# Two expert layers of a metaformer block: weights moved to the stationary side of TensorE, pooled tokens to the moving side

## What is computed

```
probs = softmax(logits, axis=1)                       # over the tokens
vals, idx = top_k(probs.transpose(0, 2, 1), K)        # each expert takes 8 tokens
pooled = einsum('bked,bke->bed', gathered, topv)      # one vector of 64 per image and expert
h = concatenate([pooled.transpose(1, 0, 2), ones], -1)
h = gelu(einsum('ebd,edh->ebh', h, weight1))          # weight1 is (32, 65, 256), last row the bias
h = concatenate([h, ones], -1)
out = einsum('ebh,eho->ebo', h, weight2)              # weight2 is (32, 257, 64), last row the bias
outputs = scatter_add(weighted by topv)
```

## Time and profile before

| | us |
|---|---|
| median of 3 runs | 206.62 (203.53 to 207.08) |
| the profiled execution | 206.30 |
| its span, first to last instruction | 204.5 |
| mean granted TensorE clock in it | 0.981 of full |
| first product of layer 1 | 178.23 |
| first `o_n` (line 918) | 186.37 |
| last DVE add ends (line 930) | 197.7 |

### The profile page before, as it was taken

One profiled execution on the slowest core, in us unless ns is written; L12 is line 12 of the kernel. 1 busy time (PEld: TensorE's weight loads), 2 busy tenths in 40 slices (PEclk: granted clock), 3 DMA queues, 4 the chain that ended last, 5 costly groups with the idle time before them and its releaser, 6 DMA issues.

```text
span 204.5 us, 10877 instructions
## 1 busy us (share of the span) xinstructions
PE 178.7 (87%) x4687; PEld 147.9 (72%) x4687; DVE 164.3 (80%) x605; ACT 109.9 (54%) x266; POOL 125.5 (61%) x113
## 2 busy tenths in 40 slices
PE   1789996999999989999999999999997988998900
PEld 1578875799869978987999798888874776684200
DVE  0768797999999898899889968888889999445960
ACT  2373435665666555667556566666457696640000
POOL 4443549598987989698898899579248930000000
PEclk9999999999999999999999999999999999999975
DMA  4955090422423143251441342432180131000896
GB/s 104 186 111 109 10 199 11 107 58 58 102 59 84 33 104 103 62 103 33 133 108 34 83 106 58 118 98 56 53 194 19 51 107 51 6 3 8 232 350 235
DMA packets 29120, 19.12 MB, mean 94 GB/s; under 512 B 2464, under 2 KB 28048, under 8 KB 29072
## 3 DMA queue, kind: packets, MB, share of 16 engines
q1 hardware_dynamic: 27440, 15.87, 31.1%
q10 hardware_dynamic: 1632, 2.56, 4.1%
HBM read 14.12 MB, written 4.30 MB: 90 GB/s over the span
## 4 chain that ended last, share of the span: by engine, by line
PE 63%; DVE 18%; issue 5%; POOL 4%; DMA 2%; ACT 2%; SPq 1%; DVEq 0%; POOLq 0%
PE ps L946 42%; PE ps L937 10%; PE ps L1006 4%; POOL r L404 3%; DMA w_rows<-in_L_conv_w_stos 2%; PE ps L1073 2%; DVE ps L715 2%; DVE tail_room L930 2%; DVE xtok L930 2%; DVE lg L871 2%; DVE x_split L866 2%; DVE st L674 2%; DVE cands L860 1%; PE ps L1194 1%; PE ps L1238 1%
## 5 line engine op out<-in xcount | busy, mean ns | idle before, releaser
L946 PE MATMUL ps<-x_split,w_hi 64*64 64x256 f16 x1000 | 50.3, 273 | 2.0 <-DVE fc L718 1.1
L382 POOL TENSOR_TENSOR xc<-xc,h 128x256 f32<-128x256 f32 x31 | 22.6, 728 | 22.8 <-DVE h_lo L699 22.8
L946 PEld LDWEIGHTS ps<-x_split,w_hi 64*64 64x64 f16 x1000 | 25.9, 107 | 13.5 <-issue 8.7
L715 DVE TENSOR_TENSOR ps<-sg_i,ps 64x256 f32<-64x256 f32 x62 | 26.6, 430 | 8.8 <-ACT ps L515 7.3
L946 PE MATMUL ps<-h_hi,w_lo 64*64 64x256 f16 x750 | 32.4, 272 | 0.8 <-issue 0.8
L946 PE MATMUL ps<-h_lo,w_hi 64*64 64x256 f16 x750 | 32.2, 272 | 0.0
L946 PE MATMUL ps<-h_hi,w_hi 64*64 64x256 f16 x750 | 32.1, 272 | 0.0
L499 ACT ACTIVATE ps<-ps,bias 128x256 f32<-128x256 f32 x32 | 14.3, 448 | 32.8 <-PE ps L946 32.8
L404 POOL TENSOR_TENSOR r<-v,pow_exp 128x16 f32<-128x16 f32 x7 | 20.6, 2936 | 8.5 <-DVE v L668 8.5
L946 PE MATMUL ps<-x_split,w_lo 64*64 64x256 f16 x500 | 24.9, 270 | 0.0
L937 PE MATMUL ps<-ident,xc 128*128 128x128 f32 x128 | 18.5, 289 | 6.9 <-DMA xc<-in_x 5.4
(11 more groups left out here) (130 smaller groups left out, 329.8 us busy)
## 6 DMA issues: line engine op xcount, KB each, us to landing
xc<-in_x SPq DMA_DIRECT2D x14, 256.0 KB, 4.0
rb_xr<-scratch SPq DMA_DIRECT2D x14, 256.0 KB, 4.4
w1s<-in_L_ffn_weight SPq DMA_DIRECT2D x8, 256.0 KB, 3.6
w2s<-in_L_ffn_weight SPq DMA_DIRECT2D x8, 256.0 KB, 3.2
rbf<-scratch SPq DMA_DIRECT2D x24, 64.0 KB, 2.4
out<-xtok SPq DMA_DIRECT2D x4, 256.0 KB, 5.4
out<-xtok ACTq DMA_DIRECT2D x4, 256.0 KB, 5.9
out<-tail_room SPq DMA_DIRECT2D x3, 256.0 KB, 4.4
```

The lines of the kernel that those rows point to most:

```text
L382: p.tensor_tensor(here, here, h32[:, i % 2, :].rearrange("p (b w) -> p b w", w=W), ALU.add) \
L715: v.tensor_tensor(ps_ig[half(h), :], sg_i[half(1 - h), :], pre[G][half(1 - h), 0:COLS], ALU.mult) \
L946: ins = pe.matmul(pre[gate][to, 0:COLS], w[half(h), tap, C * GATE_ORDER[gate]:][:, 0:C], data[half(h)], start=first and m == 0, stop=s_don ...
```

## The change

- **Layer 1** (line 1198 of the changed kernel): an expert's weights, 64 rows by 128 columns (every second one of the 256 hidden units, `m::2`), are loaded; its 16 pooled tokens move. 64 products instead of 32. The hidden values come out already turned: hidden unit on the partitions.
- The gelu writes straight into `hid_t`, 128 x 256 at a time for two halves' worth of experts. No turns of the hidden values and no DVE copies follow.
- **Layer 2** (line 1205): the weights, 128 rows by 64 columns, are loaded; 16 hidden columns move. The 16 products of one k (8 experts) all write the same 64 partitions, `half(k % 2)`; the next k writes the other 64.
- Both biases are products with `row_expert` moving (`first_bias`, now 128 columns, and the new `second_bias`); `b2`, its turn and its copy are gone.
- Pooled tokens are copied in two parts: groups 0 to 2 by ACT from one bank, group 3 by DVE from another. `pool_t` is no longer padded; its zeroing on POOL becomes a zeroing of `o_t`.
- DVE copies layer 2's result to `o_t` in four parts, and the four last turns become four products with `ident2` (two stacked 64 x 64 identities, made on POOL), which add up the two halves.
- SP issues the loads of `b1_rows` and `b2_rows`, now four each, after the LSTM and ahead of the last five pieces of expert weights.

```diff
             for g in range(NG):
                 if g == NG - 1:
                     first_bias(0)
                 pe.wait_ge(s_centered, 3 * g + 3)
-                ins = turn(PT_BANK[0:C, 128 * g:128 * g + 128], pooled[:, g, :], 128)
-            ins.then_inc(s_pooled_turned, 1)
+                ins = turn(PT_BANKS[g // (NG - 1)][0:C, 128 * (g % (NG - 1)):][:, 0:128], pooled[:, g, :], 128)
+                if g > 1:
+                    ins.then_inc(s_pooled_turned, 1)
             first_bias(1)
+            second_bias()
...
-            pe.wait_ge(s_pool_t, 2)
+            pe.wait_ge(s_pool_t, 4)
             for a in range(2):
...
-                            ins = pe.matmul(HID_BANKS[k][E * j:E * j + E, H * m:H * m + H], pool_t[half(r), e, :],
-                                            w1s[half(r), e, :], start=False, stop=m == 1)
...
+                for n in range(E // 4):
+                    for m in range(2):
+                        for r in range(2):
+                            e = E // 4 * a + n
+                            ins = pe.matmul(HID_BANKS[2 * a + r][:, 128 * m + B * n:][:, 0:B], w1s[half(r), e, m::2],
+                                            pool_t[half(r), e, :], start=False, stop=n == E // 4 - 1 and m == 1)
+                ins.then_inc(s_hidden, 1)
             for k in range(4):
                 pe.wait_ge(s_gelu, k + 1)
-                for m in range(4):
-                    ins = turn(HT_BANKS[k][:, 128 * m:128 * m + 128],
-                               hid[:, 2 * k + m // 2, m % 2::2], 128)
-                ins.then_inc(s_hid_turned, 1)
...
+                for n in range(E // 4):
+                    for m in range(2):
+                        ins = pe.matmul(O_BANKS[k // 2][half(k % 2), B * n:B * n + B], w2s[:, E // 4 * k + n, m, :],
+                                        hid_t[:, k, m, n, :], start=False, stop=n == E // 4 - 1 and m == 1)
+                ins.then_inc(s_o, 1)
+            pe.wait_ge(s_o_t, 4)
             for g in range(NG):
-                ins = turn(OB_BANK[:, C * g:C * g + C],
-                           o_t[:, QUAD * g:QUAD * g + QUAD, :].rearrange("p i e -> p (i e)"), C)
+                ins = pe.matmul(OB_BANK[:, C * g:C * g + C], o_t[:, QUAD * g:QUAD * g + QUAD, :].rearrange("p i e -> p (i e)"),
+                                ident2[:, :], start=True, stop=True)
```

More of the change, by code:

```diff
@@ L163, in metaformer, with turned_pool, pool_cols @@
         IDLE_BANK = psum[2]
-        PT_BANK = psum[6]
+        PT_BANKS = psum[6:8]
         HID_BANKS = psum[0:2] + psum[4:6]
-        HT_BANKS = psum[2:4] + psum[6:8]
-        O_BANKS, OT_BANKS, OB_BANK = psum[0:2], psum[4:6], psum[0]
+        O_BANKS, OB_BANK = psum[2:4], psum[0]
         Y_BANKS = psum[6:8] + psum[2:4] + [psum[1]] + psum[4:6] + [psum[0]]
+        def turned_pool(r, last):
+            cols = PT_BANKS[last][0:C, 0:128 if last else 128 * (NG - 1)]
+            return cols.rearrange("p (i a r n) -> p r a n i", a=2, r=2, n=E // 4)[:, r, :, :, :]
+        def pool_cols(r, last):
+            images = slice(QUAD * (NG - 1), B) if last else slice(0, QUAD * (NG - 1))
+            return pool_t[half(r), :, images].rearrange("p (a n) i -> p a n i", a=2)
         def ps_weights(n):
@@ L350, in _ @@
                     spread_r0(t + 2)
+            for k in range(4):
+                q.dma_start(b1_rows[E * k:E * k + E // 4, :], w1[E // 4 * k:E // 4 * k + E // 4, C, :]).then_inc(s_b_in, DMA)
+                q.dma_start(b2_rows[E * k:E * k + E // 4, :], w2[E // 4 * k:E // 4 * k + E // 4, H, :]).then_inc(s_b_in, DMA)
             for n in range(piece, 16):
@@ L463, in _ @@
                 else:
-                    p.memset(pool_t[:, :, :], 0.0).then_inc(s_pool_room, 1)
+                    p.memset(o_t[:, :, :], 0.0).then_inc(s_o_room, 1)
+                    p.tensor_tensor(ident2[:, :], ident[:, 0:C], ident[:, C:2 * C], ALU.add).then_inc(s_o_room, 1)
             for n, part in enumerate(LAST_R):
@@ L598, in _ @@
                 rows = slice(E * k, E * k + E)
-                a.activation(row_expert[rows, :, :], ident[rows, E * k:E * k + E // 4].unsqueeze(2).to_broadcast([E, E // 4, E]),
+                a.activation(row_expert[rows, :, :], ident[rows, E * k:E * k + E // 4].unsqueeze(2).to_broadcast([E, E // 4, B]),
                              ACT.Copy).then_inc(s_row_expert, 1)
@@ L635, in _ @@
             a.wait_ge(s_pooled_turned, 1)
-            a.wait_ge(s_pool_room, 1)
             for r in range(2):
-                a.activation(pool_t[half(r), :, 0:B].rearrange("p (a n) i -> p a n i", a=2),
-                             PT_BANK[0:C, :].rearrange("p (i a r n) -> p r a n i", a=2, r=2, n=E // 4)[:, r, :, :, :],
-                             ACT.Copy).then_inc(s_pool_t, 1)
+                a.activation(pool_cols(r, 0), turned_pool(r, 0), ACT.Copy).then_inc(s_pool_t, 1)
             for k in range(4):
-                a.wait_ge(s_hidden, k + 1)
-                a.activation(hid[:, 2 * k:2 * k + 2, :].rearrange("p q h -> p (q h)"), HID_BANKS[k][:, :], ACT.Gelu) \
+                a.wait_ge(s_hidden, k // 2 + 1)
+                a.activation(hid_t[:, k, :, :, :].rearrange("p k n i -> p (k n i)"), HID_BANKS[k][:, 0:H], ACT.Gelu) \
                     .then_inc(s_gelu, 1)
[L645 to L648, removed]
             for n, part in enumerate(FIRST_PARTS):
@@ L904, in _ @@
                                        pooled[:, g, :], ALU.mult, ALU.add).then_inc(s_centered, 1)
+            v.wait_ge(s_pooled_turned, 2)
+            for r in range(2):
+                v.tensor_copy(pool_cols(r, 1), turned_pool(r, 1)).then_inc(s_pool_t, 1)
+            v.wait_ge(s_o_room, 2)
             for k in range(4):
[L906 to L915, removed]
+                v.wait_ge(s_o, k + 1)
+                v.tensor_copy(o_t[half(k % 2), :, E // 4 * k:E // 4 * k + E // 4],
+                              O_BANKS[k // 2][half(k % 2), 0:128].rearrange("p (n i) -> p i n", i=B)).then_inc(s_o_t, 1)
             v.wait_ge(s_o_blocks, 1)
@@ L1038, in between @@
                     pe.wait_ge(s_gate_centered, 4)
-                    turn(ps_lg[:, 256:256 + 2 * E], gw_rows[:, :], 2 * E)
-                    turn(ps_lg[0:C, 384:384 + E], b2_rows[:, :], E).then_inc(s_gate_turned, 1)
+                    turn(ps_lg[:, 256:256 + 2 * E], gw_rows[:, :], 2 * E).then_inc(s_gate_turned, 1)
                 if i == 1 and t > 1:
@@ L1168, in _, with columns, second_bias @@
             pool(3)
-            pe.wait_ge(s_b1_in, 4 * DMA)
+            pe.wait_ge(s_b_in, 8 * DMA)
             pe.wait_ge(s_row_expert, 4)
+            def columns(k):
+                return row_expert[E * k:E * k + E // 4, :, :].rearrange("p n i -> p (n i)")
             def first_bias(m):
                 for k in range(4):
-                    pe.matmul(HID_BANKS[k][:, H * m:H * m + H],
-                              row_expert[E * k:E * k + E // 4, QUAD * m:QUAD * m + QUAD, :].rearrange("p j i -> p (j i)"),
-                              b1_rows[E * k:E * k + E // 4, :], start=m == 0, stop=False)
+                    pe.matmul(HID_BANKS[k][:, 128 * m:128 * m + 128], b1_rows[E * k:E * k + E // 4, m::2], columns(k),
+                              start=m == 0, stop=False)
+            def second_bias():
+                for k in range(4):
+                    pe.matmul(O_BANKS[k // 2][half(k % 2), 0:128], b2_rows[E * k:E * k + E // 4, :], columns(k),
+                              start=True, stop=False)
             for g in range(NG):
@@ L1188, in _ @@
             for a in range(2):
[L1189 to L1193, removed]
-                            ins = pe.matmul(HID_BANKS[k][E * j:E * j + E, H * m:H * m + H], pool_t[half(r), e, :],
-                                            w1s[half(r), e, :], start=False, stop=m == 1)
-                        if m == 1:
-                            ins.then_inc(s_hidden, 1)
+                for n in range(E // 4):
+                    for m in range(2):
+                        for r in range(2):
+                            e = E // 4 * a + n
+                            ins = pe.matmul(HID_BANKS[2 * a + r][:, 128 * m + B * n:][:, 0:B], w1s[half(r), e, m::2],
+                                            pool_t[half(r), e, :], start=False, stop=n == E // 4 - 1 and m == 1)
```

39 lines of the change are left out of this document (12 added, 27 removed).

## The result

The changed kernel takes 226.16 us (median of 6 runs, 224.33 to 226.65) against 205.26 (median of 6, 203.53 to 207.08): 1.103 times the kernel before, with a 95% interval of 1.098 to 1.109. The forecast was 212.7 with a range of 209.5 to 222.0. The direction was right, the size was not. The profiled execution has a span of 223.4 us against 204.5, so 18.9 us are to be found.

What follows compares the result with a forecast made beforehand. A chain of layers, turns and an add up to o_n was taken to bound the kernel; layer 1 at 7.7, layer 2 at 5.4 and smaller terms put o_n 6.4 us later: 206.3 + 6.4 = 212.7 us, range 209.5 to 222.

Steps and rivals of the forecast that it cites:

- What bounds: From layer 1 to o_n a pure chain of 8.1 us; its gain or loss reaches the end in full.
- Layer 1's round: Layer 1: loads of 128 columns set 64 rounds of 0.120 us, 7.7 us against 1.96 before.
- Layer 2: Second layer: 128 loads, each k partly overlapping the next, 5.4 us between 3.6 and 7.2, against 1.92 before.
- Ahead of layer 1: Before the first product: earlier copies and smaller bias products start layer 1 at 177.9 instead of 178.23, 0.3 us earlier.
- Behind layer 2: After layer 2: DVE's copy about 0.28 us, then four last products 1.07 us, up to o_n.
- the sum: Terms from layer 1's start at 177.9 put o_n at 192.76 against 186.37, 6.4 us later.
- rival 3: The granted clock falls at about 183 because thin work counts little, slowing both layers and scatter: about 223 us; chance 0.17.
- Rival 1: Loads do not bind in either layer; each takes 2.0 us, 202.9 us in total; chance 0.06.
- Rival 2: Strided product loads take twice as long: layer 1 13.8 us instead of 7.7, total 218.8 us; chance 0.15.
- The rule on loads and row groups: Skill page: loads overlap running matmuls only in another row group; layer 2 would take 8.6, the whole 1.4 to 3 more.
- Edits at nothing: SP's moved bias loads, DVE's dropped b2 copy and POOL's extra add, outside the layers, counted as no change.

Runs made afterwards that it cites:

- e1: The changed kernel with layer 1's products moving 128 columns instead of 16, the tokens set among zeros, same loads: 216.9 us (one run).
- e2: The changed kernel with padded moves in both layers, 128 columns in layer 1 and 64 in layer 2 instead of 16: 213.9 us (one run).
- e6: e5 with layer 1's loads reading adjacent columns instead of every second one: 209.6 us (median of 4), 1.022 times the kernel before.
- e9: The changed kernel with only layer 2 padded to 64 moved columns, layer 1 still moving 16: 219.7 us (one run).
- e3: The changed kernel with layer 2's products of two k, which write different column halves, alternating; moves stay at 16: 219.8 us (one run).
- e5: The changed kernel with the changes of e2 and e3 together: 210.5 us (median of 4), 1.026 times the kernel before.
- e4: The changed kernel with loads split into strips of 32 columns, 256 products in layer 1 and 128 in layer 2, two k alternating: 223.4 us (one run).
- e7: e5 with layer 1's loads split into two strips of 64 columns, each moving 64 columns: 210.9 us (one run).

## Why the prediction was right or wrong

- **What bounds** was right: the stretch is a chain, and what it lost, the end lost in full, with 1.3 us more behind `o_n`.
- **Layer 1's round**, 0.120 us at full clock: right (0.119 in e1, and the same count of matmuls in the changed kernel before its clock fell). That the stride does not double a product's load was right: 7.8 us against the 7.7 of the forecast in e1 and e2, and 0.4 us from e6.
- **Layer 2** was mis-sized. I took 5.4, the middle between full and no overlap of one k with the next. At full clock it took 7.14 (e2), the strict end. Rows 7 had shown an overtaking of six; the result shows about four, and a whole k would have needed 32.
- **Ahead of layer 1**: 0.2 us gained against 0.3. **Behind layer 2**: the copy 0.28 as worked out, the last products 1.1 at full clock (e2) as worked out.
- **At full clock**, from layer 1's first product to `o_n`, the sum was 192.76 - 177.9 = 14.9 us against 16.4 in e2; layer 2 alone is 1.7 too low. In its total e2, at 213.9, is near the forecast's 212.7.
- **The step that failed** is the premise that the granted clock stays full through both layers: every term of the sum behind 177.9 is priced at full clock, and "the clock falls" was kept as rival 3, at 0.17. The runs show in its place that the clock fell to half at 179.9, 2.6 us into layer 1, and stayed there to 207: layer 1 took 11.7 us instead of 7.7, layer 2 12.6 instead of 5.4, the last products 1.98 instead of 1.07. With more columns moving and the same loads it did not fall (e1, e2). I had seen that only 13 ns in 120 move data, and no row of the kernel before had thin work in it to decide by. Rival 3 had the mechanism, but the 183 of its pricing rests on no row, and it used a layer 2 that was too short; with its own 223 us it was the nearest to 226.2. The range, cut at 222, left it out. The Trainium skill's page "TensorE: Matmul & The Clock Gate", section on the clock gate, calls the throttled state the default and says that activity releases it. That agrees with e1, e2 and e9: loads alone, with TensorE busy the whole time by the profile, did not hold it.
- **Rival 1** (loads do not bind) fell: layer 1's round at full clock is the same with 16 and with 128 moved columns, and e3 against the changed kernel, like e5 against e2, changes only the order of layer 2's loads and nearly halves its time. **Rival 2** fell with e1, at 0.119 a round, and e6 prices the stride. Its counter-argument had a slip: of the 24 loads in rows 9 I read the shortest, 181 ns, where the median is 230. The conclusion stands, since contiguous loads of 64 columns at half clock (line 1205) have 179 at the shortest and 227 in the middle.
- **The rule on loads and row groups.** The same page of the Trainium skill, in its section on packing small matmuls, has it that a load overlaps with running matmuls only in another row group; the section also speaks of a background weight buffer as a second way. In e1 loads of 0.107 to 0.118 and moves of 0.107 in the same 64 rows went by in 0.119 a round. If they could not overlap, it would be over 0.21. The trace decides against the "only" here.
- **Edits at nothing** (SP's loads, POOL, DVE): nothing in the runs speaks against them. Whether the 0.7 us by which the turn of group 3 came earlier is from them was not tried; in the profiles of the experiments it starts between 175.4 and 177.4 (e6 and e4), so 0.7 lies within what these profiles differ by.

## What to carry to other kernels

With few vectors for each weight matrix, compare the columns loaded with the columns moved for each tile: the longer of the two is the round, and narrow tiles that take many columns of weights past a small stationary side keep both small. A change that thins out what moves must also be priced at half clock, for all that follows until products that move more bring it back (in layer 2 of e9, in the scatter of the changed kernel); a busy share of 100% is no assurance. If such products cannot be avoided, let them move zeros up to the length of the load (64 and 128 columns here), and let neighbours in the program write different column parts.

## What was not expected of the hardware

TensorE can run out of its own instructions. Pairs of load and matmul at 9 to 11 ns each (e4) or 17 (e7) stop after 115 and then each 128 pairs for 1.3 to 2.5 us, with instructions arriving at about 128 pairs in 3.3 to 3.7 us. The kernel before shows no such gap, although its layer 2 issues 128 pairs in 2 us. From layer 1 to `o_n` it has 64 + 16 + 128 + 8 + 4 = 220 pairs in 8.1 us, 37 ns each, which is slower than the 28 ns at which they arrive; that this is why it escapes is an estimate and was not tried. Splitting products into smaller ones thus stops paying at about 28 ns a pair over a stretch.

Adding work made the kernel 12 us faster: e2 moves 4 to 8 times as many columns as the changed kernel and takes 213.9 us against 226.2. The rounds at full clock are the same in both, so the difference is the clock's.
